# Dense relational aggregation in two float32r halves, in chunks of 4 tiles: a graph network of 6250 nodes on one core

## The reference

```python
# L0: two SAGE convolutions
def _sage_conv(x, src, dst, Wl, bl, Wr):
    agg = segment_sum(x[src], dst) / maximum(degree, 1)
    return agg @ Wl.T + bl + x @ Wr.T
# L1: three relational convolutions
def rgcn_conv(x, src, dst, etype, W, root, bias):
    seg = dst * R + etype
    agg = segment_sum(x[src], seg) / maximum(count of seg, 1)   # n x R rows
    return einsum('nrd,rdk->nk', agg.reshape(n, R, -1), W) + x @ root + bias

x = layernorm(x + L0(x))                      # 128 features
h = concatenate([x, node_emb[node_type]])     # 256 features
h = relu(rgcn_conv(h, W1)); h = relu(rgcn_conv(h, W2)); h = relu(rgcn_conv(h, W3))
x = layernorm(x + h)
```

## Time and profile before

| | us |
|---|---|
| median of 3 runs (6039.24 to 6044.68) | 6040.76 |
| the profiled execution, its own time | 6035.35 |
| its span in the profile | 6033.5 |

### The profile page before, as it was taken

The page is one execution under the profiler, slowest core; times in us unless marked ns, Lnnn a source line. Parts: engine busy times, 40 slices in busy tenths (PEclk is TensorE's granted clock), DMA queues, the critical chain, the costliest instruction groups (busy, mean ns, idle before and its releaser), DMA issues. The chain is left out here.

```text
span 6033.5 us, 91554 instructions
## 1 busy us (share of the span) xinstructions
PE 4630.4 (77%) x34588; PEld 2926.8 (49%) x34588; DVE 2966.5 (49%) x7467; ACT 1296.2 (21%) x2385; POOL 3583.5 (59%) x3576
## 2 busy tenths in 40 slices
PE   2798999976666666666665558888888798999888
PEld 1466666643333333333333335555555455555555
DVE  6898861137788888787783221222212212222222
ACT  2566640013334343343341000000000000000000
POOL 5000000027777777777777747777777677777776
PEclk6799999987778878877886669999999899999999
DMA  3223226544444444454453335655656555555554
GB/s 90 111 107 138 107 107 230 218 167 134 130 138 140 131 141 138 129 146 134 122 149 110 114 129 158 198 189 176 195 158 197 184 161 169 165 163 166 169 158 124
DMA packets 428453, 903.90 MB, mean 150 GB/s; under 512 B 71170, under 2 KB 335116, under 8 KB 406124
## 3 DMA queue, kind: packets, MB, share of 16 engines
q0 software_dynamic: 169216, 348.44, 21.1%
q1 hardware_dynamic: 126580, 450.83, 20.6%
q10 hardware_dynamic: 132216, 98.74, 5.2%
HBM read 692.22 MB, written 205.05 MB: 149 GB/s over the span
## 5 line engine op out<-in xcount | busy, mean ns | idle before, releaser
L1402 POOL DMA_INDIRECT messages<-table,src_rows x2552 | 2584.3, 1013 | 853.7 <-issue 752.0
L1453 PE MATMUL couple_bank<-slices,pieces 128*128 128x384 fp8e4 x10290 | 1809.3, 333 | 0.0
L1453 PEld LDWEIGHTS couple_bank<-slices,pieces 128*128 128x128 bf16 x10290 | 1006.3, 100 | 653.1 <-issue 65.7
L1691 DVE TENSOR_TENSOR sums<-sums,bank 128x120 f32 x873 | 236.5, 271 | 1861.6 <-PE bank L1415 1799.4
L1415 PE MATMUL bank<-group_hot,messages 128*128 128x120 bf16 x10476 | 790.8, 233 | 460.4 <-DMA messages<-table,src_rows 302.4
L1402 POOL DMA_INDIRECT messages<-table,rel_rows x940 | 914.4, 973 | 342.4 <-issue 279.7
L1415 PEld LDWEIGHTS bank<-group_hot,messages 128*128 128x128 bf16 x10476 | 697.3, 107 | 677.6 <-issue 582.4
L1679 DVE TENSOR_SCALAR rel_hot<-couple_bank,rel_dense 128x490 bf16<-128x490 f32 x1344 | 952.5, 709 | 0.0
L1561 ACT CAST stage<-couple_bank 128x980 fp8e4<-128x980 f32 x672 | 656.1, 976 | 1110.4 <-PE couple_bank L1431 1109.2
L1431 PE MATMUL couple_bank<-rel_hot,lo_dense_hot 128*128 128x490 bf16 x1344 | 477.8, 444 | 457.5 <-ACT stage L1561 320.2
L1383 POOL IOTA iota_rel_i<- 128x250 int32 (+1 forms) x2 | 1.5, 776 | 1182.6 <-DMA table<-typed_rows 1182.6
(11 more groups left out here) (269 smaller groups left out, 3696.0 us busy)
## 6 DMA issues: line engine op xcount, KB each, us to landing
slices<-relations_d SPq DMA_DIRECT2D x70, 1200.0 KB, 5.7
slices<-relations_d SPq DMA_DIRECT2D x70, 1152.0 KB, 5.5
adjacency_d<-adjacency SPq DMA_DIRECT2D x15, 4704.0 KB, 14.5
adjacency<-adjacency_d SPq DMA_DIRECT2D x15, 4704.0 KB, 14.9
relations_d<-stage ACTq DMA_DIRECT2D x84, 500.0 KB
messages<-table,src_rows POOLq DMA_INDIRECT x2552
relations_d<-stage ACTq DMA_DIRECT2D x84, 480.0 KB
inverse<-inverse_d SPq DMA_DIRECT2D x52, 640.0 KB, 5.0
```

The costliest lines, as they stand in the source:

```text
L1402: pool.indirect_dma_start(messages[:, i % MESSAGES, t, 0:ROWS[v]], None, GATHERED[v], bass.IndirectOffsetOnAxis(ap=rows[:, e:e + 1], axis= ...
L1453: mm = pe.matmul(bank[DENSE_BANKS[K % 2]][:, 0:CHUNK], pieces[M % PIECE_RING][:, tile % PIECE_TILES, piece * P:(piece + 1) * P], slice_of_ ...
L1691: vec.tensor_tensor(sums[:, ds(base, GROUP_COLS)], sums[:, ds(base, GROUP_COLS)], from_bank[:, 0:GROUP_COLS], ALU.add).then_inc(sums_added, 1)
```

## The change

The dense part works in other sizes and in another number format; the gathered part keeps its three bfloat16 pieces.

- 28 dense tiles instead of 21: 7 chunks of `DENSE_TILES = 4`, 512 columns. The second and third convolution gather 21 tiles, 177 groups. 896 couples, 112 stages.
- The source rows for the dense part get their own DRAM tables `dense_2`, `dense_3`: two float32r halves a row, a high one (rounded by ScalarE's copy into a float32r tile) and the rest (`table_halves`, `h2_halves`). A task is 49 x 2 = 98 matmuls of 128x512, both operands float32r.
- ScalarE expands the fp8 adjacency to float32r, two tiles in one copy of up to 1024 columns: a lot, 25 lots a task, in a ring of `LOT_RING = 3` buffers (`expand`). TensorE waits for `lots_by_act`, ScalarE for `dense_marks`, now counted once a tile. Slices are four a task (13, 12, 12, 12 tiles).
- To make room in SBUF: `MESSAGES` 6 to 3, `LEAD` 4 to 2, block ring 8 to 7. x1 goes to DRAM chunk by chunk in the SAGE stage and comes back a window at a time (`first_x1`).
- Couples are spread over nearly all of the first convolution (896 over some 796 half ticks), and a stage is stored in four transfers.
- The two additions of a group in the first convolution are one over two rings (`ring`). Chunks are finished in parts of two tiles, in the second convolution five half ticks apart.

```diff
-MESSAGES = 6
+MESSAGES = 3
+HALVES = 2
+DENSE_ROW = HALVES * FEAT
+DENSE_TILES = 4
+DENSE_COLS = DENSE_TILES * P
-SLICE_TILES = (25, 24)
+SLICE_TILES = (13, 12, 12, 12)
-PIECE_RING = PIECE_BLOCKS + 1
-TASK_STEPS = NODE_TILES * PIECES
+PIECE_RING = PIECE_BLOCKS
+TASK_STEPS = NODE_TILES * HALVES
+LOT_TILES = 2
+LOT_RING = 3
...
-            length = 12 if conv == 0 else 9
+            length, spacing = ((12, 12), (8, 5), (9, 9))[conv]
...
-        LEAD = 4
+        LEAD = 2
...
+        BUILD_HALVES = PLANS[0].half_ticks - 2 * (REL_TICK + 1) - 4
+        couple_half = lambda j: 2 * (REL_TICK + 1) + j * BUILD_HALVES // COUPLES
...
+        def expand(engine, copy, lot):
+
+            n, first, end = LOTS[lot % TASK_LOTS]
+            J = lot // TASK_LOTS * SLICES + n
+            engine.wait_ge(slice_in[J % 2], 16 * (J // 2 + 1))
+            if lot >= LOT_RING:
+                engine.wait_ge(dense_marks, tiles_by_lot(lot - LOT_RING))
+            of_slice = slices[:, J % SLICE_RING, 0:SLICE_TILES[n] * DENSE_COLS].rearrange("p (s h d) -> p s h d", s=CHUNK_STAGES, d=STAGE_NODES)
+            to = lots[lot % LOT_RING][:, 0:end - first, :, :].rearrange("p h s d -> p s h d")
+            return copy(to, of_slice[:, :, first:end, :])
...
-                sp.dma_start(pieces[M % PIECE_RING][:, :, :], rows.rearrange("(t p) f -> p t f", p=P)).then_inc(piece_in[M % 3], 16)
+                rows = dense_2[nodes, r * DENSE_ROW:(r + 1) * DENSE_ROW] if v == 1 else dense_3[nodes, :]
+                sp.dma_start(pieces[M % PIECE_RING][:, :, :].bitcast(f32), rows.rearrange("(t p) f -> p t f", p=P)).then_inc(piece_in[M % 3], 16)
...
-                mm = pe.matmul(bank[DENSE_BANKS[K % 2]][:, 0:CHUNK], pieces[M % PIECE_RING][:, tile % PIECE_TILES, piece * P:(piece + 1) * P],
-                               slice_of_chunk[:, :, within * STAGE_NODES:(within + 1) * STAGE_NODES], start=(at == 0), stop=(at == TASK_STEPS - 1))
+                mm = pe.matmul(bank[DENSE_BANKS[K % 2]][:, 0:DENSE_COLS], pieces[M % PIECE_RING][:, tile % PIECE_TILES, half * P:(half + 1) * P],
+                               lots[lot % LOT_RING][:, within, :, :].rearrange("p s d -> p (s d)"), start=(at == 0), stop=(at == TASK_STEPS - 1))
...
                     for b, at_r, count in ((0, 0, 3), (1, 3, 2)):
-                        op = act.copy(rows[:, at_r:at_r + count, 0, :], TABLES_1[b].rearrange("p (r f) -> p r f", f=P))
+                        act.copy(rows[:, at_r:at_r + count, 0, :], TABLES_1[b].rearrange("p (r f) -> p r f", f=P))
+                        op = act.copy(halves[:, at_r:at_r + count, 0, :], TABLES_1[b].rearrange("p (r f) -> p r f", f=P))
...
+                    for lot in lots_at[v].get(half, []):
+                        expand(act, act.copy, lot).then_inc(lots_by_act, 1)
...
-                    vec.tensor_tensor(type_sums[:, ds(base, GROUP_COLS)], type_sums[:, ds(base, GROUP_COLS)], from_bank[0:NODE_TYPES, TYPE_COLS:TYPE_COLS + GROUP_COLS], ALU.add)
-                vec.tensor_tensor(sums[:, ds(base, GROUP_COLS)], sums[:, ds(base, GROUP_COLS)], from_bank[:, 0:GROUP_COLS], ALU.add).then_inc(sums_added, 1)
+                    both = from_bank[:, 0:2 * TYPE_COLS].rearrange("p (k c) -> p k c", k=2)[:, :, 0:GROUP_COLS]
+                    vec.tensor_tensor(ring[:, :, ds(base, GROUP_COLS)], ring[:, :, ds(base, GROUP_COLS)], both, ALU.add).then_inc(sums_added, 1)
...
+                        op = vec.tensor_tensor(halves[:, at_r:at_r + count, 1, :], from_bank, halves[:, at_r:at_r + count, 0, :].bitcast(f32), ALU.subtract)
```

More of the change, by code:

```diff
@@ L86, with tiles_by_lot @@
 PIECE_BLOCKS = NODE_TILES // PIECE_TILES
[L87 to L93 removed]
+PIECE_RING = PIECE_BLOCKS
+TASK_STEPS = NODE_TILES * HALVES
+LOT_TILES = 2
+LOT_RING = 3
+LOTS = [(n, at, min(at + LOT_TILES, SLICE_TILES[n])) for n in range(SLICES) for at in range(0, SLICE_TILES[n], LOT_TILES)]
+TASK_LOTS = len(LOTS)
+LOT_OF_TILE = [l for l, (n, first, end) in enumerate(LOTS) for _ in range(first, end)]
+LAST_LOTS = [max(l for l in range(TASK_LOTS) if LOTS[l][0] == n) for n in range(SLICES)]
+def tiles_by_lot(lot):
+    n, _, end = LOTS[lot % TASK_LOTS]
+    return lot // TASK_LOTS * NODE_TILES + SLICE_FIRST[n] + end
+assert PIECE_BLOCKS * PIECE_TILES == sum(SLICE_TILES) == NODE_TILES and len(LOT_OF_TILE) == NODE_TILES
 class Plan:
@@ L112, in __init__ @@
         ready = [(2 * self.summed_after(w) + 1, "window", w) for w in range(self.windows)]
-        ready += [(max(e for e, task in zip(self.task_end, self.tasks) if task[0] == c) + 3, "chunk", c) for c in chunks]
+        ready += [(max(e for e, task in zip(self.task_end, self.tasks) if task[0] == c) + 3, "chunk", 2 * c + part) for c in chunks for part in range(2)]
         self.fins, self.begun, self.step_at, at = [], [], {}, 0
@@ L333, in resnorm_gnn @@
-        (rel_rows, out_rows), rel_rows_end = lay(weights_end, ("rel_rows", [P, GROUP * PLANS[1].groups], i32), ("out_rows", [P, CHUNK_TILES, P], f32))
+        assert first_x1_end <= CODES and rel_dense_end <= CODES + NODES_PADDED * 4
+        PIECE_BYTES, LOT_BYTES = PIECE_TILES * DENSE_ROW * 4, LOT_TILES * DENSE_COLS * 4
+        piece_homes = [all_end + n * PIECE_BYTES for n in range(2)]
+        lot_homes = [0, 0, all_end + 2 * PIECE_BYTES]
+        assert lot_homes[2] + LOT_BYTES <= types_end
@@ new lines, in resnorm_gnn @@
+        (slices,), slices_end = lay(types_end, ("slices", [P, SLICE_RING, SLICE_TILES[0] * DENSE_COLS], f8))
+        assert slices_end <= stage_end
+        piece_homes += [slices_end + n * PIECE_BYTES for n in range(PIECE_RING - 2)]
+        lot_homes[0:2] = [piece_homes[-1] + PIECE_BYTES + n * LOT_BYTES for n in range(2)]
+        pieces = [lay(o, (f"pieces{n}", [P, PIECE_TILES, DENSE_ROW], f32r))[0][0] for n, o in enumerate(piece_homes)]
+        lots = [lay(o, (f"lots{n}", [P, LOT_TILES, CHUNK_STAGES, STAGE_NODES], f32r))[0][0] for n, o in enumerate(lot_homes)]
@@ L1336, in conv_sync @@
                 load_block(1, m)
-            for j in range(2, SLICE_RING):
-                load_slice(1, j)
             for w in range(2):
```

297 lines of the change are left out of this document (165 added, 132 removed).

## The result

The changed kernel takes 6249.05 us (median of 4 runs, 6244.16 to 6253.24), the kernel before on the same chip 6042.19: a ratio of 1.0343, 95% interval 1.033 to 1.036. Forecast were 5870 us, in a range of 5650 to 6130, and a gain. The prediction is wrong in size and in sign.

The account below looks back on a forecast made before the run. Gathers bound the later convolutions; in the first, GpSimd, TensorE and VectorE lie within a few per cent. 6033.5 + 250 (first) - 206 (second) - 216 (third) = 5861.5 us of span, said as 5870, range 5650 to 6130.

Parts of the forecast that it names:

- What is removed; the later convolutions: Second and third convolutions: 58 groups fewer in each, periods 5.4 and 5.5 us a group, gains of 206 and 216 us.
- The dense matmul: Later convolutions: a float32r matmul of 512 columns is one pass of 0.216 us, so TensorE needs 4.82 us a group.
- rival 2: Dense matmuls, later convolutions: weight load not hidden, 0.356 us a matmul, about 6650 us in all; chance 0.04.
- the step that failed: First convolution, VectorE: 4.45 pairs of one-hots a group take 3.90 us to about 4.21, +0.31, +4.7 a window.
- two accounts of one cycle: First convolution: 97.7 us a window from couples, 95.6 from buffers; the longer holds, so 98 a window, +250 us.
- the buffers: First convolution: GpSimd fills three groups in the 22.9 us gap, then stands still about 10 us: 85.2 + 10.4 = 95.6 a window.
- The bound of +500: First convolution: upper bound on its added time if both costs, couples and buffers, add in full (108 us a window).
- 1: Dense matmuls, later convolutions: float32r streams at the float32 record's rate, 0.43 us a matmul, about 7150 us; chance 0.12.
- 3: Later convolutions: ScalarE becomes the bound at 6.0 us a group, +195, about 6060 us; chance 0.11.
- 5: First convolution hides most of its cost in the time VectorE and GpSimd idle: 5680 us; chance 0.10.
- 4: First convolution pays both costs in full, 105 to 108 us a window: about 6110 us, slower; chance 0.09.
- What would show it: Right: first-convolution windows 98 us apart, GpSimd waiting 200 us or more for TensorE. Wrong: it under 2350 or over 2700 us.

Follow-up runs that it names:

- e1: Changed kernel with the batch of one-hots moved ahead of the group's own one-hots and the ring addition: 5894 us.
- e2: Kernel before with 3 message buffers for 6 and one-hots 2 groups ahead for 4: 6177 us, +136.
- g4: e1 with two transfers a stage instead of four, same bytes, adjacency permuted: 108 us less than the 5894 us of e1.
- h2: Changed kernel with batches first, 4 message buffers, couples in two pairs of PSUM banks and the comparison row in SBUF as float32: 5655 us.
- h1: Kernel before with the comparison row in SBUF, still float32, instead of PSUM: 6023 us, 0.4% faster than before.
- g3: Kernel before with the comparison row in SBUF as float16 and couples in two pairs of PSUM banks: 6107 us, 1.0% slower.
- g2: Kernel before with the comparison row in SBUF as float16 alone: 6115 us, 1.2% slower.

## Why the prediction was wrong, point by point

- **What is removed; the later convolutions.** Right in the count and in the time: 708 gathers in each, periods of 5.38 and 5.56 us (GpSimd's first gathers) for 5.4 and 5.5, and ScalarE busy 871 us in the second for 876. That the periods fit so well is partly luck. The dense matmul was mis-sized, 0.232 us for 0.216; by the prediction's own sums TensorE then needs 0.63 + 19.4 x 0.232 = 5.13 us a group, with its finishes 5.28 in the second and 5.46 in the third, and is the slowest in both: GpSimd waits for it 95.4 and 116.6 us there. What the engines' waits on each other add is then 0.1 us a group in each, where the prediction had 0.3 and 0.35. The two misses cancel.
- **Weight loads.** The rule of the Trainium skill that rival 2 quotes stands in "TensorE: Matmul & The Clock Gate", The mechanism. It does not hold here: the loads of 0.189 us lie inside the distance of 0.232. The same section of the Trainium skill also has a load into the background weight buffer pulled ahead of running matmuls, which would allow it; no run here shows which buffer is used.
- **First convolution: the step that failed.** The prediction wrote that 4.45 pairs a group add 0.31 us to VectorE's 3.90 and put couples and batches "all along". It counted VectorE's work and not where it stands, and so kept the overlap of the earlier trace rows at no cost. For half of the batches no group stood any longer on TensorE's side between the addition's group and the couple that needs the batch. What was "two accounts of one cycle" was a third: group, addition, batch and couple one after the other, 6.40 us where about 4.2 were put down. The move was in the diff and in the loop; the working had its instructions, but not what they were moved past. Put right by itself (e1) it is worth 355 us.
- **Its other terms.** Without the order the first convolution stands at +302 (e1) for the +250 forecast, and the kernel at 5894 for 5870, inside the forecast's own range. One by one, the buffers cost 137 us in the kernel before (e2), 5.5 us a window where the prediction had 10.4, and two transfers more a stage 105 in the new order (g4), 4.2 a window for 3. With the 355 these make 597 of the 657 us, but that is no account of them: the costs were taken in different kernels and do not simply add. The transfers cost 76 in the old order, and a fourth buffer brought nothing measurable in the new one. The prediction took the longer of its two sums and not both, which e1 does not decide. The 112 batches more and the halves' window work were not run by themselves.
- **The bound of +500** was the sum of the two costs in full. It was no bound, since it too assumed that the overlap of the earlier trace rows stays.
- **Rivals.** 1, 2, 3 and 5 did not come. 4 named the right place, the right sign and the wrong mechanism, and gave 6110.
- **What would show it.** The signs worked: a first convolution over 2700 us was the stated mark of being wrong, and GpSimd waiting for TensorE 200 us or more came as 809. Windows came (2915.7 - 71.5) / 25 = 114 us apart, 71.5 being GpSimd's wait at the end, and not 98.
- **What the change is worth.** The best version with it that was run, h2, took 5655 us, 6.4% less than the kernel before; the best without it, h1, 6023. The comparison is not quite even: h1 has no second pair of banks, which brought g3 8 us at most over g2. The idea of the change was sound, and the place of half the batches hid it.

## What to carry to other kernels

When work is rescheduled on an in-order engine, write down for every moved instruction which waits now stand ahead of it, who waits for its result, and what that engine still has to do in between: equal work and buffers cost 743 us here for one half's shift. In the profile the sign is a pair of waits in opposite directions between two engines that grows (563 and 136 us before, 830 and 561 after) while neither is busy for three quarters of the stretch. And before an operation is made faster or a buffer added, ask what sets the period beside it: the half as long comparison brought 336 and 46 us in two kernels and cost 71 in a third, and a fourth buffer brought nothing or 104.

## What the runs showed of the hardware that was not expected

A float32r matmul of 512 columns is one pass of 0.232 us, 0.45 ns a column, where the 384 columns of fp8 took 0.42; the cause of the 7% is open.

The comparison of 490 columns takes 0.709 us from a float32 row in PSUM, 0.490 from a float32 row in SBUF and 0.341 from float16 in SBUF, and the gathers that GpSimd issues take 1.029, 1.055 and 1.114 us on the mean of the first convolution. The Trainium skill ("VectorE: DVE Perf Modes", Mode 2×_2P — use both read ports for one tensor) says that a one-tensor operation from SBUF can use both of VectorE's read ports, also at float32, and one from PSUM cannot; the order of the three durations agrees. The Trainium skill says ("SBUF — State Buffer", SBUF: two separate sides) that such an operation locks GpSimd out of the port pair they share, so that it cannot write the descriptors of a DMA of its own; the longer gathers, by 2.5 and 8% on the mean, agree in direction.

Beside a long operation the trace shows a full stop. Once a window VectorE scales the ring, with two float32 tensors from SBUF; in the kernel before, VectorE and GpSimd:

```profile
2526.10 2.34 DVE L1730 TENSOR_TENSOR scaled<-sums,inverse 128x1280 f32<-128x1280 f32 x1
2526.30 2.99 POOL L1402 DMA_INDIRECT messages<-table,src_rows  x1 [0.30 <-issue]
2528.37 2.44 DVE L1730 TENSOR_TENSOR type_scaled<-type_sums,inverse 3x1280 f32<-3x1280 f32 x1
2529.59 2.07 POOL L1402 DMA_INDIRECT messages<-table,src_rows  x1 [0.30 <-issue]
```

A gather that takes 0.957 us otherwise (the median) takes 2.99 and 2.07 here, and both end 0.85 us after the VectorE operation that they began under. Of 30 gathers of this convolution that begin under such an operation with 1.2 us or more of it to come, 24 end 0.83 to 0.85 us after it; the other six are held past the second operation too and take 4.4 to 5.3 us. So the small rise of the means is no sign of a partial stop: where the operation is long, the stop is as long. The sentence of the Trainium skill is about one-tensor operations, and these have two.
